# A Mamba-2 and mixture-of-experts layer on one core: the convolution's taps read from PSUM, and a masked product kept there

## What is computed

```python
zxbcdt = jnp.einsum('bld,ed->ble', xn, in_proj_w)
z, xBC, dt = ...                      # 1024, 1024 + 2 * 128, 16 columns
pad = jnp.pad(xBC, ((0, 0), (DC - 1, 0), (0, 0)))
conv = sum((pad[:, k:k + l, :] * conv_w[:, k] for k in range(DC))) + conv_b   # DC = 4
xBC = conv * jax.nn.sigmoid(conv)
xs, Bm, Cm = ...                      # 16 heads of 64, and two vectors of 128
Y_diag = jnp.einsum('bcln,bcsn,bhcls,bcshp->bclhp', Cm, Bm, Lmat, X)
Y_off = jnp.einsum('bcln,bchpn,bhcl->bclhp', Cm, states, jnp.exp(Acs))
y = (Y_diag + Y_off + D * xh) * (z * jax.nn.sigmoid(z))
x = x + jnp.einsum('bld,ed->ble', rmsnorm(y), out_proj_w)
```

## Time and profile before

| | us |
|---|---|
| median of 3 runs (6404.81 to 6410.18) | 6409.54 |
| the profiled execution | 6412.97 |
| its span, first to last instruction | 6411.1 |
| of it: 219.6 to 3219.0, the mixer's loop from its first to its last L723 | 2999.4 |
| of it: from 3400 on, the experts and the sum | 3011 |

### The profile page before, as it was taken

The page is one execution under the profiler, slowest core; times in us unless marked ns, Lnnn a source line. Parts: engine busy times, 40 slices in busy tenths (PEclk is TensorE's granted clock), DMA queues, the critical chain, the costliest instruction groups (busy, mean ns, idle before and its releaser), DMA issues. The chain is left out here.

```text
span 6411.1 us, 109995 instructions
## 1 busy us (share of the span) xinstructions
PE 5781.9 (90%) x28797; PEld 4345.1 (68%) x28798; DVE 3957.1 (62%) x10033; ACT 2733.7 (43%) x5780; POOL 3763.9 (59%) x2980
## 2 busy tenths in 40 slices
PE   2888888888888888888859999999999999999899
PEld 0556555565565565565548888888788888888787
DVE  1888888888888888888834444444344444444355
ACT  1555555555555555555513333333333333333322
POOL 0466666666666666666645555555555555555477
PEclk8899999999999999999979999999999999999999
DMA  9243343333343333333348887887877777887687
GB/s 351 107 124 119 106 131 120 111 130 107 117 136 105 119 125 105 122 122 105 129 123 194 196 217 173 213 196 175 228 155 176 186 164 179 211 214 196 106 269 256
DMA packets 338146, 1028.39 MB, mean 160 GB/s; under 512 B 55060, under 2 KB 59412, under 8 KB 337124
## 3 DMA queue, kind: packets, MB, share of 16 engines
q1 hardware_dynamic: 175512, 669.44, 30.3%
q0 software_dynamic: 145568, 321.56, 25.7%
q10 hardware_dynamic: 16816, 34.37, 1.4%
HBM read 580.45 MB, written 444.74 MB: 160 GB/s over the span
## 5 line engine op out<-in xcount | busy, mean ns | idle before, releaser
L1324 POOL DMA_INDIRECT acc_dram<-y_e,ids x576 | 907.9, 1576 | 1115.6 <-ACT y_e L1397 680.3
L1205 PE MATMUL bank<-w_hi,x_hi 128*128 (+1 forms) x2560 | 1058.0, 413 | 0.0
L1205 PE MATMUL bank<-w_hi,x_lo 128*128 (+1 forms) x2560 | 1002.3, 392 | 0.0
L1205 PE MATMUL bank<-w_lo,x_hi 128*128 (+1 forms) x2560 | 1001.5, 391 | 0.0
L938 DVE SCALAR_TENSOR_TENSOR acc<-raw,conv_w,acc 128x128 f32<-128x128 f32 x1920 | 820.3, 498 | 7.3 <-ACT acc L665 7.3
L602 POOL DMA_INDIRECT list_dram<-tok_id,pos x512 | 633.3, 1237 | 155.9 <-issue 154.6
L1415 DVE TENSOR_TENSOR h_lo<-bank,h_hi 128x256 fp32r<-128x256 f32 x576 | 243.5, 423 | 753.5 <-ACT h_hi L1386 746.8
L1397 ACT ACTIVATE y_e<-bank,xg_e 128x512 f32<-128x512 f32 x576 | 396.4, 688 | 693.4 <-PE bank L1205 649.1
L1316 POOL DMA_INDIRECT xg_e<-h_dram,ids x576 | 572.0, 993 | 195.0 <-issue 174.1
L1391 ACT ACTIVATE th_f<-bank 128x256 f32<-128x256 f32 x576 | 221.3, 384 | 1017.6 <-PE bank L1205 964.1
L770 PE MATMUL bank<-xn_t,w_in 128*128 128x128 f32 x5120 | 590.5, 277 | 66.4 <-ACT xn_t L644 66.4
(11 more groups left out here) (248 smaller groups left out, 10997.2 us busy)
## 6 DMA issues: line engine op xcount, KB each, us to landing
hi_dram<-w_hi_m SPq DMA_DIRECT2D x130, 768.0 KB, 7.4
lo_dram<-w_raw SPq DMA_DIRECT2D x130, 768.0 KB, 8.8
w_hi<-hi_dram SPq DMA_DIRECT2D x130, 768.0 KB
w_lo<-lo_dram SPq DMA_DIRECT2D x130, 768.0 KB
w_raw<-in_w_experts_dram SPq DMA_DIRECT2D x128, 768.0 KB
acc_dram<-zeros ACTq DMA_DIRECT2D x2, 16640.0 KB, 102.5
acc_c<-acc_dram SPq DMA_DIRECT2D x128, 256.0 KB, 3.5
h_dram<-h SPq DMA_DIRECT2D x64, 288.0 KB
```

Source lines behind the costliest of these rows:

```text
L1205: last = nc.tensor.matmul(acc, a, b, start=(i == 0), stop=(i == len(terms) - 1))
L1324: pool.indirect_dma_start(acc_dram[r % NACC], bass.IndirectOffsetOnAxis(ap=ids[:, r:r + 1], axis=0), y[:, r % YSLOTS, :], None, compute_op ...
```

## The change

1. **Projection with three older tokens.** `xn_t` becomes 131 tokens wide: the last three of the chunk before, multiplied by `starts` (zero at the start of a sequence), and the 128 of this one. Each of the 40 matmuls of the input projection now streams 131 columns, so that a block's 131 values lie in PSUM. The groups are 3, 3, 3 and 1 blocks, in `half(1)`, `half(0)`, `half(6)` and `half(7)`; `dt` goes to `half(7)`. The third group waits for the first exponential (`l_exp`), which reads `bank[3]`.
2. **The carry moves.** DVE's copy of the old columns is now 4 times 3 floats of `xn_t`, at the head of DVE's step, and ACT's copy of `xn_t` waits for it.
3. **No copy to `raw`.** The tile and ACT's three copies are gone. All four taps read PSUM: `acc = raw_of(i) * w + acc` on DVE has one operand in PSUM and one in SBUF.
4. **`gm` stays in PSUM**: masked in place in `half(4)`, and read from there by the two products with `lm`. The router's product, which writes into the same half, waits for them (`m_done`).
5. **Orders.** On PE `ydiag` goes ahead of the new states, and `yoff`, which writes where the last taps are read, goes behind both, with a wait for all taps and for `dt`. On ACT the last two groups of the first tap go ahead of the copy of `h2`. On DVE `dt` is read behind all taps.

The core of the diff:

```diff
-        raw = sb("raw", [P, 2, NE, TAPS - 1 + P])
+        xn_t = sb("xn_t", [P, KD, TAPS - 1 + P])
+        def raw_of(i):
+            return half((1, 0, 6, 7)[i // 3])[:, i % 3 * (OLD + P):(i % 3 + 1) * (OLD + P)]
 # ACT
-                        nc.scalar.copy(raw[:, 1 - p, 4 * g:4 * g + n, TAPS - 1:],
-                                       half(1 - g % 2)[:, 0:n * P].rearrange("p (n t) -> p n t", n=n)).then_inc(S["raw_sb"], 1)
-                            last = nc.scalar.activation(acc[:, i, :], raw[:, 1 - p, i, 0:P], ACT.Identity,
+                            last = nc.scalar.activation(acc[:, i, :], raw_of(i)[:, 0:P], ACT.Identity,
 # PE
-                                    last = nc.tensor.matmul(half(1 - g % 2)[:, i * P:(i + 1) * P], w_in[:, k, m:m + P],
+                                    last = nc.tensor.matmul(raw_of(i), w_in[:, k, m:m + P],
                                                             xn_t[:, k, :], start=(k == 0), stop=(k == KD - 1))
+                        if f is None:
+                            pe.wait_ge(S["l_exp"], 2 * c + 1)
+                        else:
+                            pe.wait_ge(S["taps"], XGROUPS * (f + 1))
+                            pe.wait_ge(S["dt_raw"], f + 1)
 # DVE
-                        tt(gm[:], half(4)[:, 0:P], tri[:], ALU.mult)
+                        tt(half(4)[:, 0:P], half(4)[:, 0:P], tri[:], ALU.mult)
-                               gm[:].unsqueeze(1).to_broadcast([P, 8, P]), ALU.mult).then_inc(S["m_done"], 1)
+                               half(4)[:, 0:P].unsqueeze(1).to_broadcast([P, 8, P]), ALU.mult).then_inc(S["m_done"], 1)
-                                        last = stt(out=acc[:, i, :], in0=raw[:, 1 - p, i, k:k + P], scalar=conv_w[:, i, k:k + 1],
+                                        last = stt(out=acc[:, i, :], in0=raw_of(i)[:, k:k + P], scalar=conv_w[:, i, k:k + 1],
                                                    in1=acc[:, i, :], op0=ALU.mult, op1=ALU.add)
```

More of the change, by code:

```diff
@@ L448, in rows_of, with group @@
             return dram[bass.ds(chunk * P, P), :]
+        def group(g):
+            return range(3 * g, min(3 * g + 3, NE))
+        def raw_of(i):
+            return half((1, 0, 6, 7)[i // 3])[:, i % 3 * (OLD + P):(i % 3 + 1) * (OLD + P)]
         def heads(t, n=NH, w=HD):
@@ L642, in step @@
                         act.wait_ge(S["xnT_ps"], f + 1)
[L643 to L644 removed]
+                        act.wait_ge(S["carry"], f + 1)
+                        nc.scalar.copy(xn_t[:, :, OLD:], half(0).rearrange("p (k t) -> p k t", k=KD)).then_inc(S["xnT_sb"], 1)
                     if t is not None:
@@ L763, in step @@
                         at_least(pe, S["gz_done"], 2 * f)
[L764 to L768, removed]
+                        for g in range(XGROUPS):
+                            if g == 2 and c is not None:
+                                pe.wait_ge(S["l_exp"], 2 * c + 1)
+                            for i in group(g):
+                                m = DI + i * P
                                 for k in range(KD):
-                                    last = nc.tensor.matmul(half(1 - g % 2)[:, i * P:(i + 1) * P], w_in[:, k, m:m + P],
+                                    last = nc.tensor.matmul(raw_of(i), w_in[:, k, m:m + P],
                                                             xn_t[:, k, :], start=(k == 0), stop=(k == KD - 1))
-                            if g == 2:
+                            if g == XGROUPS - 1:
                                 for k in range(KD):
-                                    last = nc.tensor.matmul(half(1)[:, 2 * P:2 * P + NH], xn_t[:, k, :],
+                                    last = nc.tensor.matmul(half(7)[:, 2 * P:2 * P + NH], xn_t[:, k, OLD:],
                                                             w_in[:, k, DIN - NH:DIN], start=(k == 0), stop=(k == KD - 1))
@@ L783, in step @@
                     if c is not None:
[L785 to L790, removed]
                         pe.wait_ge(S["btok_sb"], c + 1)
@@ L795, in step @@
                         pe.wait_ge(S["h2T_sb"], t + 1)
+                        if c is not None:
+                            pe.wait_ge(S["m_done"], 2 * c + 2)
                         for k in range(KD):
@@ L799, in step @@
                         last.then_inc(S["rt_ps"], 1)
+                    if c is not None:
+                        pe.wait_ge(S["x1s_done"], c + 1)
+                        pe.wait_ge(S["m_done"], 2 * c + 2)
+                        for hh in range(NH):
+                            last = nc.tensor.matmul(bank[1][:, hh * HD:(hh + 1) * HD], lm[:, hh * P:(hh + 1) * P],
+                                                    x1s[:, hh * HD:(hh + 1) * HD], start=True, stop=True)
+                        last.then_inc(S["ydiag_ps"], 1)
                     if c is not None:
@@ L883, in step @@
                 def step(e, f, c, t, q, p, ws):
+                    if f is not None:
+                        at_least(dve, S["z_ps"], 2 * f)
+                        ts(xn_t[:, :, 0:OLD], xn_t[:, :, P:P + OLD], col(starts, f), None, ALU.mult).then_inc(S["carry"], 1)
                     def series(n):
```

71 lines of the change are left out of this document (28 added, 43 removed).

## The result

The changed kernel takes 6438.89 us (median of ten runs, 6419.09 to 6448.84), the kernel before 6409.45 beside it. The ratio is 1.0044, with a 95% interval of 1.0033 to 1.0054: slower by 0.4%, where 6236 us was forecast. The profiled execution took 6440.98 us, its span is 6439.2.

The account below looks back on a forecast made before the run. Bound: the mixer's cycle through DVE's long run, slowed by GpSimd's products, with PE's stream next. Gain 1.9 us per step, 4.0 with the clock up, taken as 2.8; times 62, 174 us off 6412.97, less 3.4: 6236, range 6160 to 6340.

Parts of the forecast that it names:

- DVE's parts: Mixer step on DVE: taps 4.5 us less, mask products 1.3 less; taps and `dt` end 5.8 us earlier.
- The slower rival: Taps from PSUM cost more: gain gone at 0.42 us each, 6565 us in all at 0.5; chance 0.09.
- PE's stream: PE from projection to `yoff`, the next bound: DVE waits for `yoff`, leaving 1.9 us gain per step.
- a step with the clock up: Output projection keeps full clock in each step: 4.0 us gain per step, 6162 us; rival's chance 0.14.
- The step that failed: PE at the router: nothing fills the wait for ACT's `h2` copy, which ends at 1539.0, after PE at 1538.3.
- The part on the clock: Output projection loses 2.4 us per step at low clock; the change leaves one 2.4 us wait ahead of it.
- falls in some steps and not in others: Clock at the output projection: 2.8 us gain per step, between 1.9 and 4.0; 6195 to 6290, chance 0.45.
- PE's 1.00 us wait at the projection: PE's wait at L770: said not to drop the clock.
- those for being right: Taps near 0.34 us, mask products near 1.2, L956 waiting for `yoff`, 2 to 3 us before ranking, projection 7.1 to 9.5.
- those for being wrong: PE waits for taps at `yoff`; projection well over 9.4 us; or `h2` copy over 1 us late, `hn` awaiting GpSimd.
- The sum: Mixer loop: 2.8 us gain per step, times 62 is 174 us, giving 6236 us.

Follow-up runs that it names:

- the filler in both: Eight unused 64-column products between `h2` transposes and router, in the changed kernel (6224.79 us) and in the kernel before with the changed kernel's PE order (6391.51 us).
- one version (35 of 51 steps for 16): Changed kernel with states ahead of `ydiag`, `h2` transposes ahead of the projection's last block and ACT's `h2` copy ahead of its last first tap: 6236.91 us.
- another (29 of 51 for 5): Changed kernel with `yoff` back between `h2` transposes and router, trading PSUM tiles with `ydiag`, which goes last: 6127.34 us, ratio 0.9559.
- the narrow filler's kernel: Changed kernel plus eight unused 64-column products on PE between the `h2` transposes and the router: 6224.79 us, ratio 0.9716.

## Why the prediction was wrong

**DVE's parts were right.** Taps forecast 8.4 us, measured 7.83; mask products 2.4, measured 2.35; `dt`'s second instruction lost half of its wait, 0.59 us for 1.04. The PSUM operand does keep the taps and the mask products out of GpSimd's way. The rule of the Trainium skill that spoke against the change (Perfetto Trace Analysis, Optimizing Scalar/DVE Operations: about 125 ns of access on PSUM, about 60 on SBUF) does not show here: a tap from PSUM costs 0.26 us, five from SBUF with GpSimd quiet 0.28 each. The slower rival rested on taps at 0.42 us or more; slower it became, but not by that.

**PE's stream was right in work and wrong in clock.** The projection was forecast at 9.4 us and takes 9.27. From the projection's start to `yoff`'s end the forecast has 1547.1 - 1527.7 = 19.4 us. In the changed kernel's 13 steps without any fall it is 19.6 on average, up to the start of `z` behind `yoff`; in the step shown, with the fall, 1553.1 - 1528.6 = 24.5. That `yoff` would be late and not the taps was right, and so was the size of a step with the clock up: 47.6 - 4.0 = 43.6 forecast, 43.9 to 44.2 measured in the 13 steps without any fall.

**The step that failed** is the sentence "Before, `yoff` filled the wait for ACT's copy of `h2`; now nothing does." It was priced as a wait of 0.7 us (measured 1.04) and nothing more. Its price is the clock behind it: 3.3 us on `ydiag`, 1.3 on the states and 0.4 on the router, all on the path, since DVE waits for `yoff`. The part on the clock looked only at the pause ahead of the output projection, which the change shortens; it never asked where the change opens a new one. The forecast there, falls in some steps and not in others, came true (16 of 51). It also read PE's 1.00 us wait at the projection as harmless. There that was so, and in the changed kernel the 46 steps with a wait of 1.1 us at the projection keep their clock on it (five with 2.1 us or more lose it). But behind `dt` and `h2`'s small products a wait of about 1 us is not harmless: 37 of 51 steps fall. The signs that the prediction named show the gap. Each of those for being right was seen, from the taps' 0.34 us to the wait of 2.41 us ahead of the ranking, and of those for being wrong only the long projection, in these five steps: none of the signs looked at PE's clock between the router and `z`.

**The sum.** Forecast 2.8 us less per step, measured 0.6 more: 3.4 x 62 = 211 us, against a miss of 6439 - 6236 = 203. The 37 steps include 16 that also fall on the output projection, which the forecast had, and 4 on the input projection (one of them on both). The 18 that fall in the middle alone take 48.8 us on average, 4.8 more than the 44.0 of those without any fall, and 37 in 51 of that is 3.5 us per step. Without it the step of 48.2 would be 44.7, where the forecast's mean was 47.6 - 2.8 = 44.8. The missing term accounts for the miss; that the rest agrees so closely is in part luck, since 2.8 was a choice between 1.9 and 4.0.

**What stays open:** why 14 of 51 steps keep their clock behind the same wait of about 1 us. The rows show the fall and the work ahead of it, not what decides. That the small products ahead of the wait matter is read from comparing two places in the step; no run varied them.

## What to carry to other kernels

When an edit takes work off TensorE's queue between two waits, price not only the wait but the clock behind it: look for places where the engine has just done small work and then stands, and see what runs next and who waits for that. Refill such a place with the kernel's own work, here by trading two PSUM tiles; where there was none, 1.9 us of unneeded products per step were worth 214 us. And compare versions with the same wait filled in both before judging the edit itself: the same edit measured 29 us worse, or 167 us better with the filler in both.

## What was not expected of the hardware

- About a microsecond of standing cost ten microseconds at half the clock: granted 0.52 in the stretch from 1540.2 to 1550.3.
- Curing a fall in one place can leave more of them at another pause: on the output projection in one version (35 of 51 steps for 16), on the input projection in another (29 of 51 for 5). In the narrow filler's kernel it did not: 43 of 51 steps have no fall.
- Eight products of 64 columns held the clock as well as two of 512: 6224.79 and 6225.12 us.
